# Attention with layer norm and a routed low-rank FFN on one Trainium2 core: the low-key term of both heads in one matmul, for a pair's first two units

## The reference

```
xn  = (x - mean) / sqrt(var + 1e-5)                    over the last axis
q, k, v = einsum(xn, Wq), einsum(xn, Wk), einsum(xn, Wv), with biases
att = softmax(causal(q k^T / 8)) / 8
z   = (att v) reshaped to (b, s, 1024)
out = x + z @ proj + ffn(xn)
ffn(xn) = xn @ W.T + the low-rank product (rank 1, 2, 4 or 8) of the expert that
          the router picks for the token, times its softmax weight
```

## Time and profile before

| what | before |
|---|---|
| median of 3 runs | 1383.08 us (1381.21 to 1384.03) |
| the profiled execution | 1382.88 us |
| its span, first to last instruction | 1381.1 us |
| TensorE busy | 1362.9 us, 11053 matmuls |
| weight loads of TensorE busy | 1160.4 us, 11053 |
| VectorE busy | 1119.5 us |
| ScalarE busy | 1076.7 us |
| GpSimd busy | 971.5 us |

### The profile page before, as it was taken

How to read it: one execution, slowest core, us unless ns; L and a number is a source line. 1 busy time by engine, 2 the same in 40 slices (tenths; PEclk the granted TensorE clock), 3 DMA queues, 4 the chain that set the end, 5 groups by cost and what they waited for, 6 DMA issues and landing times.

```text
span 1381.1 us, 35107 instructions
## 1 busy us (share of the span) xinstructions
PE 1362.9 (99%) x11053; PEld 1160.4 (84%) x11053; DVE 1119.5 (81%) x4015; ACT 1076.7 (78%) x3161; POOL 971.5 (70%) x1421
## 2 busy tenths in 40 slices
PE   6999999999999999999999999999999999999998
PEld 5788888888888888888888888888888888888887
DVE  6988878888787887879788787887878878787784
ACT  4787877878877787787778778777887877878784
POOL 5777766777766777667777667776676777677664
PEclk9999999999999999999999999999999999999999
DMA  5444454544445445444544544444454444445441
GB/s 128 109 115 103 112 124 93 119 117 104 108 111 120 101 105 123 111 108 104 119 108 106 122 104 108 111 116 112 96 123 113 101 115 114 117 93 118 109 105 47
DMA packets 112691, 150.88 MB, mean 109 GB/s; under 512 B 18239, under 2 KB 47230, under 8 KB 112510
## 3 DMA queue, kind: packets, MB, share of 16 engines
q1 hardware_dynamic: 111646, 148.36, 45.4%
q10 hardware_dynamic: 864, 0.29, 0.1%
HBM read 10.69 MB, written 4.19 MB: 11 GB/s over the span
## 4 chain that ended last, share of the span: by engine, by line
PE 95%; DVE 2%; POOL 1%; issue 1%; ACT 1%; DMA 0%; ACTq 0%; DVEq 0%; POOLq 0%
PE zp L1261 21%; PE ptp L1237 20%; PE scores L1225 13%; PE jobp L1123 12%; PE scores L1228 11%; PE outp L1273 6%; PE jobp L1128 6%; PE jobp L1138 1%; PE outp L1282 1%; DVE prob L932 1%; POOL prob L597 1%; PE jobp L1143 1%; PE jobp L1133 0%; PE jobp L1298 0%; PE outp L1287 0%
## 5 line engine op out<-in xcount | busy, mean ns | idle before, releaser
L597 POOL TENSOR_TENSOR prob<-prob,rden 128x128 f32<-128x128 f32 (+3 forms) x1024 | 712.8, 724 | 352.2 <-DVE rden L921 350.2
L932 DVE CUSTOM_DVE_ANT_0 prob<-scores,mask 128x128 f32<-128x128 f32 (+3 forms) x1024 | 465.2, 488 | 213.5 <-issue 192.2
L682 ACT ACTIVATE prob<-prob,nmax 128x128 f32<-128x128 f32 (+3 forms) x1024 | 564.8, 556 | 35.4 <-DVE nmax L932 35.3
L1237 PE MATMUL ptp<-ident,prob 128*128 128x128 f32 x2560 | 370.0, 274 | 1.5 <-DVE pt L944 0.8
L1225 PE MATMUL scores<-k_twice,q_parts 128*128 128x128 f32 (+3 forms) x1024 | 331.3, 333 | 4.8 <-DMA k_twice<-k_hi 2.5
L1228 PE MATMUL scores<-k_low,q_parts 128*128 128x128 f32 (+3 forms) x1024 | 321.7, 323 | 0.0
L1237 PEld LDWEIGHTS ptp<-ident,prob 128*128 128x128 f32 x2560 | 294.7, 141 | 30.2 <-issue 7.2
L1261 PE MATMUL zp<-pt,v_sb 128*64 128x64 f32 (+3 forms) x4096 | 307.7, 303 | 0.2 <-ACT pt L693 0.2
L693 ACT ACTIVATE pt<-ptp 128x128 f32<-128x128 f32 (+3 forms) x512 | 221.0, 432 | 109.8 <-PE ptp L1237 109.8
L1261 PEld LDWEIGHTS zp<-pt,v_sb 128*64 128x64 f32 x4096 | 221.4, 137 | 51.7 <-issue 19.5
L1225 PEld LDWEIGHTS scores<-k_twice,q_parts 128*128 128x128 f32 x1024 | 192.8, 188 | 72.6 <-issue 47.6
(11 more groups left out here) (179 smaller groups left out, 1701.0 us busy)
## 6 DMA issues: line engine op xcount, KB each, us to landing
k_twice<-k_hi SPq DMA_DIRECT2D x508, 128.0 KB, 2.3
q_parts<-q_lo SPq DMA_DIRECT2D x256, 128.0 KB, 2.5
q_parts<-q_hi SPq DMA_DIRECT2D x254, 128.0 KB, 2.3
xin<-in_L_attn_x_dram SPq DMA_DIRECT2D x16, 256.0 KB, 3.8
xres<-in_L_attn_x_dram SPq DMA_DIRECT2D x16, 256.0 KB, 3.1
out_dram<-osb SPq DMA_DIRECT2D x15, 256.0 KB, 2.6
pt<-in_L_attn_Wq_dram SPq DMA_DIRECT2D x1, 512.0 KB, 4.8
pt<-in_L_attn_Wk_dram SPq DMA_DIRECT2D x1, 512.0 KB, 5.8
```

Source lines behind the costliest of these rows:

```text
L597: nc.gpsimd.tensor_tensor(part, part, scale, ALU.mult).then_inc(pn_ready, 1)
L682: nc.scalar.activation(part, part, ACT.Exp, bias=nmax[:, s % NROT, h:h + 1], scale=-1.0, accum_out=den[:, s % NROT, h:h + 1]).then_inc(p_r ...
L932: nc.vector.tensor_tensor_reduce(out=prob[:, s % NROT, h, 0:cols], in0=scores[h][:, 0:cols], in1=mask[:, S - cols:S], scale=-INV_SCALE, sc ...
L1237: done = nc.tensor.transpose(ptp[h][:, P * j:P * j + P], prob[:, s % NROT, h, P * j:P * j + P], ident[:])
```

## The change

In a pair's first and second unit (`s % NBLK < 2`), `narrow_scores` replaces the four matmuls by three. The first has q_hi of both heads as its weights and k_low of both heads as its columns: 2 x 128 columns in the first unit, 2 x 256 in the second. Since k_low[h] is zero outside head h's own rows, the columns of head h get q_hi k_lo of head h. Then each head's q_parts x k_twice is added onto its own half of the columns. Both heads of such a unit lie side by side in one bank: `scores[0]` in the first unit, `scores[1]` in the second (`place`).

Waits change with it. The first unit waits until VectorE has read `scores[0]` for the fourth unit before (`head(s - 1, 0)`), and no longer for `scores[1]`. The second waits for head 1 of unit s - 2, which was the last to use `scores[1]`. The third unit's head 0 waits for the first unit's head 1, its head 1 for the second unit's. VectorE's maximum of either head in a narrow unit waits for both heads' scores, since they share a bank. The wait for `own_copied` stays only where it means something, once at the start.

```diff
--- before.py
+++ after.py
@@ -201,6 +201,12 @@
 def width(s):
 
     return P * (s % NBLK + 1)
+
+
+def place(s, h):
+
+
+    return (s % NBLK, width(s) * h) if s % NBLK < 2 else (h, 0)
 
 
 def build(nc, x, Wq, bq, Wk, bk, Wv, bv, proj, W, Wp, bp, sim, temp, Wd, Wu, out):
@@ -923,14 +929,15 @@
             def maximum(c, s):
                 cols = width(s)
                 for h in range(2):
-                    scored, turned = c.fixed(c.head(s, h)), c.fixed(c.head(s - NROT, h))
+                    bank, first_col = place(s, h)
+                    scored, turned = c.fixed(c.head(s, 1 if s % NBLK < 2 else h)), c.fixed(c.head(s - NROT, h))
 
                     dve.wait_ge(consts_ready, 3)
                     dve.wait_ge(s_ready, scored)
 
                     wait(dve, t_ready, turned)
                     nc.vector.tensor_tensor_reduce(
-                        out=prob[:, s % NROT, h, 0:cols], in0=scores[h][:, 0:cols], in1=mask[:, S - cols:S],
+                        out=prob[:, s % NROT, h, 0:cols], in0=scores[bank][:, first_col:first_col + cols], in1=mask[:, S - cols:S],
                         scale=-INV_SCALE, scalar=HUGE, op0=ALU.add, op1=ALU.min,
                         accum_out=nmax[:, s % NROT, h:h + 1]).then_inc(sm_ready, 1)
 
@@ -1211,17 +1218,35 @@
                     done = nc.tensor.matmul(outp[:, 0:E], bvt[:], projs[:, n, :], start=n == 0, stop=n == NPAIR - 1)
                 done.then_inc(bias_bank_ready, 1)
 
-            def score(c, s):
+            def narrow_scores(c, s):
+
+
+                i, p = s % NBLK, s // NBLK
+                cols, queries = width(s), slice(P * i, P * i + P)
+
+                wait(pe, sm_ready, c.head(s - 1, 0) if i == 0 else c.head(s - 2, 1))
+                nc.tensor.matmul(scores[i][:, 0:2 * cols].rearrange("p (h k) -> p h k", k=cols), q_hi[:, p % 2, queries],
+                                 k_low[:, :, p % 2, 0:cols], start=True, stop=False, skip_group_check=True)
+                for h in range(2):
+                    nc.tensor.matmul(scores[i][:, cols * h:cols * h + cols], q_parts[:, h, p % 2, queries],
+                                     k_twice[:, h, p % 2, 0:cols], start=False, stop=True,
+                                     skip_group_check=True).then_inc(s_ready, 1)
+
+            def score(c, s, first):
                 i, p = s % NBLK, s // NBLK
                 if i == 0:
 
-                    pe.wait_ge(own_copied, 4)
+                    if first and p == 0:
+                        pe.wait_ge(own_copied, 4)
                     pe.wait_ge(qk_moved[p % 2], c.moved(p))
                     pe.wait_ge(low_padded, c.values(p, 1))
+                if i < 2:
+                    narrow_scores(c, s)
+                    return
                 queries = slice(P * i, P * i + P)
                 for h in range(2):
 
-                    wait(pe, sm_ready, c.head(s - 1, h))
+                    wait(pe, sm_ready, c.head(s - 1, h) if i == 3 else c.head(s - 2 + h, 1))
                     nc.tensor.matmul(scores[h][:, 0:width(s)], q_parts[:, h, p % 2, queries],
                                      k_twice[:, h, p % 2, 0:width(s)], start=True, stop=False)
 
@@ -1300,7 +1325,7 @@
 
             def step(c, s, first=False, last=False, tail=False):
                 if not tail:
-                    score(c, s)
+                    score(c, s, first)
                 if first and s == 0:
                     later()
                 unit = due(s, LAG_T, 1, first, tail)
```

## The result

| | before | changed |
|---|---|---|
| median of 7 runs | 1382.94 us (1381.20 to 1384.03) | 1378.41 us (1376.78 to 1379.63) |
| the profiled execution, its span | 1382.88, 1381.1 us | 1376.78, 1375.0 us |
| TensorE's matmuls | 11053 | 10797 |
| from a unit 0 to the next batch's unit 0, mean | 84.21 us | 83.90 us |

The ratio is 0.9967 [0.9957, 0.9977]: faster by 0.33%, or 4.5 us, where 0.86%, or 11.8 us, was forecast. The 256 matmuls that are gone are one for each of 16 batches x 16 narrow units.

The account below looks back on a forecast made before the run. TensorE, 99% busy, was taken as the bound. Per batch 0.33 (units 0, 4, 20) + 0.48 (8, 28, 24) - 0.05 (12, 16) - 0.02 (29) = 0.74 us, times 16 11.8: 1371.1 us, range 1360.0 to 1377.0.

Parts of the forecast that it names:

- First unit, undisturbed.: Score matmuls of a pair's first unit, as in unit 4: 0.40 us becomes 0.29, saving 0.11, since weight loads set the pace.
- Second unit, 0.00: Score matmuls of a pair's second unit: 0.47 us before and after, as a 256-column matmul lasts as long as a load.
- The maxima: VectorE's maxima in narrow units wait for both heads, starting 0.59 and 0.77 us after the unit's start, 0.12 and 0.24 later.
- Units 12 and 16: VectorE's run without idle time from unit 12 to 16: unit 12's 0.11 is lost and unit 16 ends 0.05 us later.
- The copy's end to the released start, 0.14 us: From the end of VectorE's copy of the transposes' bank to head 1's transposes in unit 16: 0.14 us, bounds 0.11 and 0.18.
- Unit 24 ... Saving 0.16.: First unit 24: VectorE's copy ends at 756.36, so head 1's transposes start at 756.50 in place of 756.66, saving 0.16 us.
- Units 8 and 28 ... Saving 0.16 each.: First units 8 and 28: scores go from 0.45 to 0.29 us, head 1's transposes not held by VectorE's copy.
- On that cover I cost it at nothing.: VectorE's later maxima are hidden by its idle time ahead of the third unit's maximum, 1.44 us in unit 18: cost 0.
- rival 4: VectorE becomes the bound: delayed maxima push the fourth unit's scores, every pair loses 0.36 us, 1429 us; chance 0.05.
- rival 3: Weight loads aren't the pace: undisturbed units stay at 0.40 us and only waits go, 1378.7 us, or 1382.9; chance 0.09.
- Rival 1: All waits go, unit 16's too: eight first units fall from 3.72 to 2.32 us a batch, 1360.5 us; chance 0.10.
- Rival 2: The run through units 12 to 16 costs more: -0.36 us a batch in place of -0.05, 1376.1 us; chance 0.14.

Follow-up runs that it names:

- Experiment 2: Changed kernel's banks and waits, but with the old four matmuls, each head having its own two, all in one bank: 1385.02 us, ratio 1.0019.
- Experiments 5 and 6: Changed kernel with the statistics' aggregation in step 11 instead of 13 (5): 1372.07 us; changed kernel with unit 12 alone as before the change (6): 1375.98 us.
- experiment 1: Changed kernel with only a pair's first unit merged, the second unit's four matmuls in two banks again: 1375.75 us, ratio 0.9957.
- Experiment 3: Changed kernel, with ScalarE's copy of head 0's transposes ahead of q_hi in step 8 alone: 1376.42 us, ratio 0.9957.
- experiment 9: Changed kernel with ScalarE's copy first in step 8, later casts in step 24, earlier aggregation, and step 26's z_lo behind unit 27's maximum: 1363.12 us, ratio 0.9851.
- experiment 10: Changed kernel with ScalarE's copy first in steps 8 and 28, later casts in step 24 and earlier aggregation: 1366.86 us, ratio 0.9879.
- experiment 4: Changed kernel, with GpSimd's k_low casts of step 24 waiting until VectorE has made xt_lo: 1372.71 us, ratio 0.9933.

## Why the prediction was wrong

Right, by its own steps:

- **First unit, undisturbed.** Three matmuls take 0.29 us, as rebuilt (starts at 0, 0.12 and the transposes at 0.29). Units 0, 4 and 20 with their successors gave 0.37 for a forecast of 0.33: 0.11 in the first unit and 0.01 in the second. Experiment 2, with 16.62 for these units again, shows that it is the matmul taken away that does it.
- **Second unit, 0.00** for TensorE: 0.465 for 0.476 before. A moving operand from two heads' rows goes at the pace of one.
- **The maxima**, 0.59 and 0.77 after the start, were measured as forecast, and the idle time in unit 18 stayed over 1 us (1.34).
- **Units 12 and 16.** The wait moved behind the scores as forecast, and unit 12's 0.11 is lost. The stretch ends 0.02 later in most batches and 0.07 on the mean (0.05 forecast). Experiments 5 and 6 confirm the mechanism: without unit 12's change the stretch is as long as before, and with a shorter run 0.37 is gained.
- **The copy's end to the released start, 0.14 us**: 0.15 in unit 16 and 0.14 in unit 9.

- **"Unit 24 ... Saving 0.16."** Step 24 fell by 0.14. Where only the first unit is merged (experiment 1), units 24 to 26 keep 0.13 of it. In the changed kernel it is lost in step 26 (+0.18), by the second of the two steps below.

Wrong, and together 0.47 of the forecast's 0.74 us a batch:

- **"Units 8 and 28 ... Saving 0.16 each."** The scores did fall by 0.16, from 0.45 to 0.29. What failed is that I followed the transposes' bank of head 1, which VectorE copies, in the same unit, and not that of head 0, which ScalarE copies, in the next. ScalarE's copy of unit 5 ends at a time that doesn't move with TensorE, and was already just in time: with 0.14 from its end to the start that it releases, 716.37 gives 716.51 where the transposes started at 716.53. The margin of 0.02 could have been read before the change. Experiment 3 gives the 0.14 back in unit 9, experiment 9 in unit 29. For unit 29 I had looked at q_lo alone and put 0.02 on it; experiment 10 shows that q_lo's limit lies close too, but it wasn't the first one.
- **"On that cover I cost it at nothing."** The cover of the third unit's maximum was read in unit 18. Unit 26 has none: its maximum stands behind xq_lo and xt_lo, a run of VectorE work without idle time that starts when ScalarE has made xq_hi. The delay of unit 25's maximum came through by another way than the rival 4 had it: not as 0.24 us of lateness, but through k_lo to GpSimd's casts, which slid over xq_lo and stretched it by 0.20 us. That cost 0.18 in units 24 to 26 (-0.16 forecast, +0.02 measured). Experiment 1 takes it back by undoing the second unit, experiment 4 by moving the casts.

What is missing from the forecast's 0.74 is then 0.15 (unit 9) + 0.14 (unit 29) + 0.18 (unit 26) + 0.02 (unit 16, on the mean) = 0.49, less 0.04 gained over forecast in the undisturbed units and 0.02 in the others: 0.43 = 0.74 - 0.31.

By its time alone the result would fit **rival 3**, loads that aren't the pace, with 1378.7 us. The traces exclude that: unit 4's three matmuls stand where the forecast had them. Of the Trainium skill's page "TensorE: Matmul & The Clock Gate", section "Back-to-back issue gap", the rule that spoke against the change thereby doesn't hold for these matmuls: four and three of them differ by 0.11 us here, where the rule has 0.003. The same section says that its formula leaves the weight load out, which the prediction should have read with it, and gives about 81 ns for a 128-column matmul with its load; the rows here have 100. **Rival 1** fell with the waits that stayed. **Rival 2** had the right place and the wrong price: 0.02 to 0.07 for its 0.36. **Rival 4** didn't occur as a whole, yet its chain, from the second unit's maximum to the fourth's scores, ran in one pair of eight, on 0.20 us of stretching.

## What to carry to other kernels

Where TensorE is 99% busy, a gain on it arrives only up to the next fixed date of another engine. So for every unit in which a saving falls, list what its own and the next unit's matmuls wait for from each engine, with the margin between that date (its end plus the measured 0.14 us) and the present start; the 0.02 us in unit 9 was such a margin, and the dates that the forecast had missed in units 9, 26 and 29 took 0.47 of its 0.74 us. And read a cover in the place where it is needed, not in one that looks like it: the idle time of unit 18 said nothing of unit 26. A merge that hardly shortens the bounding engine's work (the second unit's here: 0.09 a batch gained, 0.16 lost) isn't free either, if it delays the reader.

## What the runs showed of the hardware

- **VectorE's xq_lo (two SBUF operands) and GpSimd's casts of k_low hold each other up.** xq_lo takes 0.69 us alone (experiment 4), 0.95 with 0.41 of overlap, 1.15 with 0.60, and ends 0.54 to 0.55 after the casts in both: it loses the overlap less 0.15. In the fifth batch of the kernel before it is the other way round:

```profile
425.08 0.69 DVE L811 TENSOR_TENSOR xq_lo<-xt,xq_hi 128x512 fp32r<-128x512 f32 x1 [0.80 <-ACT xq_hi L657]
425.69 1.10 DVE L827 TENSOR_TENSOR xt_lo<-xt,xt_hi 128x512 fp32r<-128x512 f32 x1
```

```profile
424.41 1.83 POOL L561 CAST k_low<-k_lo 64x512 fp32r<-64x512 f32 x2 [0.41 <-DVE k_lo L819]
```

There the second cast and xq_lo start within 0.002 us of each other, xq_lo takes its 0.69, and the cast takes 1.17 in place of 0.60. The xt_lo behind it then overlaps the cast for 0.56 and takes 1.10 in place of 0.68. The changed kernel's fifth batch has xq_lo 0.71, a cast of 0.96 that starts 0.22 after it, and xt_lo 1.09. In all these rows but for the tie the one that starts later is held up; no experiment set that order on purpose. The Trainium skill's page "SBUF — State Buffer", section "Who interferes with whom", has VectorE's second port pair shared with GpSimd under an exclusive lock; that agrees with these rows. VectorE's z_lo, which reads one operand from PSUM, took 0.67 to 0.69 even where GpSimd ran beside it for 0.7 us.
- **One matmul of 256 columns with a moving operand in two runs of rows** is followed 0.12 us later by the next (700.91 to 701.03), like one of a single run; with 512 columns 0.24 later (702.35 to 702.59), where a job's 512 columns take 0.23.
